# A routed feed-forward and attention kernel: scratch rows ordered by partition, gates of the last blocks worked out in block 6, block 1 turned inside block 0

## The chip, the cores and the metric

The kernel runs on one core of one Trainium2 chip. The metric is the device time of one launch in microseconds (us); each kernel was run several times and the median stands for it. The profile is one further execution.

Engines: TensorE (PE in the rows; PEld is its weight load), VectorE (DVE), ScalarE (ACT), GpSimd (POOL), SyncE (SP). SP and ACT issue plain DMA transfers; GpSimd issues indirect ones (gathers and scatters of rows by a list of indices).

## The reference

Three layers on x of 4 x 256 tokens with 256 features: half a mixture-of-experts feed-forward, attention, and the same feed-forward again.

```
x = x + 0.5 * ffn(layernorm(x))
x = x + attention(layernorm(x))       # 16 heads of 16, causal
x = x + 0.5 * ffn(layernorm(x))

ffn: logits = x @ router.T                     # 8 experts
     the best 2 experts of each token, gates = softmax of their 2 logits
     for each expert: a, b = split(x @ w_in.T) # 2 x 512
                      o = (silu(a) * b) @ w_out.T
                      sum += gate * o
     result = sum + bias
```

## The kernel before

Tokens lie in tiles of 128 on the partitions (8 tiles, in pairs); TensorE does all products in split precision (each operand as a high and a low part, three products). A feed-forward pass `ffn(f)`, f = 0 or 1, has these stages:

1. **Normalise and store.** The normalised rows `xn` (in the `arena` tile, or `xn_late`) are stored by ACT to `xn_scratch` in memory (L696, one transfer of 1 MB, semaphore `xn_stored`). In the first pass SP has by then issued the loads of weights (four of 1 MB for `w_raw`, 4 KB rows; two of 0.5 MB for `w_out`, 1 KB rows). In memory row `i * 128 + p` is token p of tile i.
2. **Route** (DVE L879 to L973, TensorE `route`). Each of the 2048 (token, expert) pairs gets a place in 23 blocks of 128 rows, each block of one expert. One-hot tiles (`row_hot`, `blk_hot`, `blk_pair`) are multiplied on TensorE (L1267) to give the pair's number at each place; from it come `gather_row` (which signals `plan_ready`) and `scatter_row`. `past` and `block_expert` give the expert of each block. Then the gates (L960 to L964) and, for the last two blocks, `live`, `slot_token` and `gate_row` (L966 to L973, signal `slots_ready`).
3. **Blocks.** GpSimd waits for `plan_ready` and `xn_stored`, gathers the rows of four blocks ahead (L509) and goes on by one for each block; a gather into a buffer waits until TensorE has turned the block that was in it. TensorE turns a block (`turn_block`), projects it in two halves (`project`, results a and b), turns the gated product (`turn_gated`) and multiplies by the second weights (`combine`), the three of them interleaved over neighbouring blocks. ACT copies the high parts out (`copy_xT`, `silu`, `copy_gT`, `split_out`, `copy_y`), DVE the low parts (`copy_xT_low`, `gated`, `split_out_low`, `copy_gT_low`, and in the first pass `split_low` of the expert weights). GpSimd scatters each block's result to `y_scratch` (L515). SP waits for the gathers of blocks 0 and 1 before it issues more weight loads. At block 6 GpSimd adds the bias to x (L503), at block 10 it gathers the gates of the last two blocks.
4. **Adding up.** The first 21 blocks go through `y_scratch`; when the last scatter has landed, SP loads them back to `y_in` (which lies in `w_out`) with eight transfers of 256 KB, one for each pair of tiles and each choice k, L436. DVE adds rows times gate to x (`add_rows`, L1021), ACT scales others (L627) that TensorE adds through an identity (`add_scaled`, L1351) on top of the last two blocks, which it spreads by one-hot tiles (`spread`, L1337). DVE adds TensorE's sum to x (`settle`, L1032); in the first pass the layer norm for attention follows, in the second SP stores the output.

`weigh_slots`, in the diff, is new; it is called in DVE's `body`.

## Time and profile before

| | |
|---|---|
| median of 3 runs | 437.04 us (435.76 to 438.95) |
| the profiled execution | 440.74 us, of which 438.6 us are its span |
| busy share of the span | PE 93%, PEld 76%, DVE 69%, ACT 59%, POOL 56% |
| DMA | 38.90 MB, 25738 packets; HBM read 29.37 MB, written 9.19 MB |
| the chain that ended last | PE 65%, DVE 12%, DMA 10%, issue 5%, ACT 3%, POOL 2% |

Times in the rows are microseconds from the start of the span. A timeline row has the start, the duration, engine, line of the kernel, operation, what it writes and reads, and in brackets how long the engine was idle before it and what ended that. SPq and ACTq are the instruction queues that issue transfers. The first pass runs from the start to about 159, attention to about 293, the second pass to the end. DMA queue q1 is SP's, q10 ACT's, q0 GpSimd's.

### The profile page before, as it was taken

What the parts mean: (1) busy time and instruction counts of PE and PEld (TensorE: products, weight loads), DVE (VectorE), ACT (ScalarE), POOL (GpSimd) and SP (SyncE); (2) the same over time, 40 slices, a digit from 0 to 9 for tenths busy, and PEclk for the clock granted to TensorE, in tenths of its full rate; (3) what the DMA queues carried; (4) which work ended last, traced back from release to release, by engine and by line L of the source; (5) the groups of instructions that cost most, each with busy time, mean ns of one, the idle gap of its engine ahead of it and who ended that gap; (6) DMA issues with size and microseconds to landing.
All of it is one profiled execution on the core that took longest, in us unless ns stands there. A gap on an engine that the chain in (4) does not pass through costs nothing.

```text
span 438.6 us, 10176 instructions
## 1 busy us (share of the span) xinstructions
PE 408.5 (93%) x2911; PEld 333.9 (76%) x2912; DVE 300.8 (69%) x613; ACT 257.1 (59%) x638; POOL 247.7 (56%) x307
## 2 busy tenths in 40 slices
PE   7768999999999889799999999888799999999996
PEld 4536888888888867588887888764488888888884
DVE  6767996865556697777677676966365575556566
ACT  2706885555655455788787787822155655655552
POOL 5136445866467349657777577210365586754850
PEclk9679999999999999989999999996999999999999
DMA  8929931111211630000000000007551212112136
GB/s 278 371 68 347 389 100 59 47 51 60 59 48 36 190 109 1 1 1 2 4 1 0 0 0 0 1 1 252 153 184 49 62 37 72 60 48 52 44 103 208
DMA packets 25738, 38.90 MB, mean 89 GB/s; under 512 B 3056, under 2 KB 20720, under 8 KB 25712
## 3 DMA queue, kind: packets, MB, share of 16 engines
q1 hardware_dynamic: 19088, 24.41, 16.3%
q0 software_dynamic: 4544, 12.07, 9.4%
q10 hardware_dynamic: 2080, 2.10, 1.4%
q8 instruction: 14, 0.23, 0.2%
q14 instruction: 12, 0.10, 0.1%
HBM read 29.37 MB, written 9.19 MB: 88 GB/s over the span
## 4 chain that ended last, share of the span: by engine, by line
PE 65%; DVE 12%; DMA 10%; issue 5%; ACT 3%; POOL 2%; SPq 1%; DVEq 0%; ACTq 0%; POOLq 0%
PE bank L1301 24%; PE bank L1323 12%; PE bank L1459 7%; PE bank L1470 4%; PE bank L1311 3%; DMA xn_scratch<-arena 3%; PE bank L1224 3%; DMA w_out<-y_scratch 3%; PE bank L1426 2%; PE bank L1277 2%; PE bank L1506 2%; DMA arena<-xn_scratch,gather_row 2%; DVE w_lo L876 1%; DMA y_scratch<-arena,scatter_row 1%; PE bank L1460 1%
## 5 line engine op out<-in xcount | busy, mean ns | idle before, releaser
L509 POOL DMA_INDIRECT arena<-xn_scratch,gather_row x46 | 50.8, 1105 | 72.7 <-PE bank L1277 42.1
L515 POOL DMA_INDIRECT y_scratch<-arena,scatter_row x42 | 60.2, 1434 | 34.3 <-ACT arena L681 31.2
L1301 PE MATMUL bank<-w_hi,xT_hi 128*128 x184 | 62.6, 421 | 1.2 <-ACT xT_hi L640 1.2
L990 DVE TENSOR_TENSOR wo_lo<-w_out,wo_hi 128x1024 fp32r<-128x1024 f32 x46 | 60.8, 1321 | 4.1 <-PE bank L1323 1.9
L995 DVE TENSOR_TENSOR gT_lo<-bank,gT_hi 128x512 fp32r<-128x512 f32 x46 | 31.7, 689 | 39.3 <-ACT gT_hi L655 39.2
L1301 PE MATMUL bank<-w_hi,xT_lo 128*128 x184 | 58.1, 397 | 0.0
L1301 PE MATMUL bank<-w_lo,xT_hi 128*128 x184 | 57.8, 395 | 0.0
L593 POOL TENSOR_TENSOR k_head<-k_hi,head_mask 128x256 fp32r<-128x256 f32 x64 | 38.7, 625 | 29.1 <-PE bank L1460 22.2
L648 ACT ACTIVATE arena<-bank 128x512 f32<-128x512 f32 x46 | 27.5, 598 | 45.7 <-PE bank L1301 45.7
L670 ACT ACTIVATE wo_hi<-w_out 128x1024 fp32r x46 | 48.8, 1060 | 6.0 <-issue 4.1
L979 DVE TENSOR_TENSOR xT_lo<-bank,xT_hi 128x256 fp32r<-128x256 f32 x46 | 19.5, 424 | 39.0 <-ACT xT_hi L640 38.9
L1459 PE MATMUL bank<-k_head,xT_hi 128*128 128x256 f32 (+1 forms) x128 | 40.4, 397 | 1.9 <-ACT probs L778 1.2
L1301 PEld LDWEIGHTS bank<-w_hi,xT_lo 128*128 128x128 f32 x184 | 35.1, 191 | 8.0
L1301 PEld LDWEIGHTS bank<-w_lo,xT_hi 128*128 128x128 f32 x184 | 34.9, 190 | 8.2
L593 POOL TENSOR_TENSOR k_head<-k_lo,head_mask 128x256 fp32r<-128x256 f32 x64 | 38.3, 618 | 0.6 <-DVE k_lo L1105 0.6
L681 ACT ACTIVATE arena<-bank 128x256 f32<-128x256 f32 x42 | 16.2, 385 | 37.0 <-PE bank L1323 37.0
L770 ACT ACTIVATE probs<-bank,neg_max 128x256 f32<-128x256 f32 x64 | 29.9, 478 | 8.6 <-DVE neg_max L1118 8.6
L788 ACT ACTIVATE pT_hi<-bank 128x384 f16<-128x384 f32 x64 | 28.1, 487 | 11.3 <-PE bank L1470 10.5
L1323 PE MATMUL bank<-wo_hi,gT_hi 128*128 128x256 f32 x184 | 33.0, 302 | 1.4 <-ACT gT_hi L655 1.4
L1224 PE MATMUL bank<-ones 128*128 128x512 f16 x95 | 31.1, 479 | 3.3 <-POOL ident L462 1.8
L1131 DVE SCALAR_TENSOR_TENSOR pT_lo<-bank,pT_hi 128x384 f16<-128x384 f32 x64 | 32.4, 548 | 0.6
L1004 DVE TENSOR_TENSOR arena<-arena,bank 128x512 f32<-128x512 f32 x46 | 31.2, 678 | 1.0 <-issue 0.9
(180 smaller groups left out, 968.8 us busy)
## 6 DMA issues: line engine op xcount, KB each, us to landing
w_raw<-in_win_t SPq DMA_DIRECT2D x8, 1024.0 KB, 9.7
w_out<-in_wout_t SPq DMA_DIRECT2D x16, 512.0 KB, 8.0
w_out<-y_scratch SPq DMA_DIRECT2D x16, 256.0 KB, 4.9
xn_scratch<-arena ACTq DMA_DIRECT2D x2, 1024.0 KB, 8.7
x<-in_x SPq DMA_DIRECT2D x4, 256.0 KB, 3.6
out<-x SPq DMA_DIRECT2D x4, 256.0 KB, 2.1
arena<-xn_scratch,gather_row POOLq DMA_INDIRECT x46, 3.5
y_scratch<-arena,scatter_row POOLq DMA_INDIRECT x46, 3.0
```

Of the source, the lines that this page charges most:

```text
L509: pool.indirect_dma_start(out=xb[j % 2][:, :], out_offset=None, in_=xn_dram, in_offset=bass.IndirectOffsetOnAxis(ap=gather_row[:, j:j + 1] ...
L515: pool.indirect_dma_start(out=y_dram, in_=y[j % 2][:, :], in_offset=None, out_offset=bass.IndirectOffsetOnAxis(ap=scatter_row[:, j:j + 1], ...
L593: ins = pool.tensor_tensor(k_head[s % KSLOTS][:, part, hh, :], k[:, c, :].bitcast(F32), head_mask[:, h % HPC:h % HPC + 1].to_broadcast([P, ...
L670: act.activation(wo_hi[u][:, :, :], w_out[:, bass.ds(e, 1), :, :].rearrange("p o c d -> p (o c) d"), ACT.Copy)\
L990: dve.tensor_tensor(wo_lo[:, :, :], w_out[:, bass.ds(e, 1), :, :].rearrange("p o c d -> p (o c) d"), wo_hi[u][:, :, :].bitcast(F32), ALU.s ...
L995: dve.tensor_tensor(gT_lo[:, :, :], bank[4][:, :].rearrange("p (c t) -> p c t", c=HK), gT_hi[:, :, :].bitcast(F32), ALU.subtract).then_inc ...
L1004: dve.tensor_tensor(g[:, :], sa[:, :], bank[2 + u][:, :], ALU.mult).then_inc(g_done, 1)
L1131: dve.scalar_tensor_tensor(pT_lo[u][:, :, :], bank[3 + hh][:, 0:3 * P].rearrange("p (k t) -> p k t", k=3), P_SCALE, pT_hi[u][:, :, :], ALU ...
L1224: pe.matmul(bank[into][:, :], ones[:, :], bc(ones[:, :], 1, [P, 512 // P, P]), start=True, stop=True)
L1301: last = pe.matmul(bank[2 * half + u][:, :], tok[u][:, k, :], wts[:, bass.ds(e, 1), k, half * H:(half + 1) * H], start=(part == 0 and k == ...
L1323: last = pe.matmul(bank[y_bank(j)][:, 0:D], tok[:, c, :], wts[:, c, :], start=(part == 0 and c == 0), stop=(part == 2 and c == HK - 1))
L1459: pe.matmul(to, q[:, 1 if tail else 0, :], keys[:, part, :, 0:width], start=(n == 0), stop=False)
```

## The change

In words:

- Rows in `xn_scratch` and `y_scratch` are numbered by partition first (`p * 8 + i` instead of `i * 128 + p`), so a partition's 8 tiles are one run of 8 KB in memory. The store of `xn` writes such runs. `pair_id` and `tile_edge` are made to fit; `tile_edge` costs one more small operation on GpSimd among the constants.
- `y_in` is laid out by choice, then tile. A pair of tiles is loaded by one transfer of 512 KB for both choices, in runs of 2 KB; four transfers instead of eight.
- The gates, `live` and `slot_token` move out of `route` to `weigh_slots`, which DVE runs at the end of block 6. The gates in memory are ordered like the pairs, so `gate_p`, `gate_q` and `gate_row` go, and the gather of gates takes `pair_i` itself.
- In `route`, `past` comes after `blk_pair`.
- On TensorE block 1 is turned between the two halves of block 0's projection, not after them.

```diff
--- before.py
+++ after.py
...
@@ -177,7 +177,7 @@
 
         y_experts = TOPK * TILES // HK
         assert LAST + y_experts <= SCATTERED - FULL + 1 and LAST * TILES * P <= (SCATTERED - LAST * 2 - FULL + 1) * HK * D
-        y_in = view(w_out_words, LAST * HK * D, [TILES, TOPK, D])[0]
+        y_in = view(w_out_words, LAST * HK * D, [TOPK, TILES, D])[0]
 
         wr = sb("wr", [P, DK, E])
         bias_half = sb("bias_half", [P, D])
...
@@ -372,9 +369,9 @@
 
         x_rows = x_in.rearrange("b (j p) d -> p (b j) d", p=P)
         out_rows = out.rearrange("b (j p) d -> p (b j) d", p=P)
-        xn_rows = xn_dram.rearrange("(i p) d -> p i d", p=P)
-        gate_rows = gate_dram.rearrange("(p q) o -> p (q o)", p=P)
-        y_rows = y_dram[0:TOPK * T, :].rearrange("(k i p) d -> p k i d", p=P, k=TOPK)
+        xn_rows = xn_dram.rearrange("(p i) d -> p i d", p=P)
+        gate_rows = gate_dram.rearrange("(k p i) o -> p k (i o)", p=P, k=TOPK)
+        y_rows = y_dram[0:TOPK * T, :].rearrange("(k p i) d -> p k i d", p=P, k=TOPK)
 
 
         @block.sync
@@ -426,15 +423,14 @@
                     pass_on_w_out()
 
                 sp.wait_ge(slots_ready, f + 1)
-                sp.dma_start(gate_rows, gate[:, :, :].rearrange("p k i -> p (k i)")).then_inc(gates_stored, 16)
+                sp.dma_start(gate_rows, gate[:, :, :]).then_inc(gates_stored, 16)
 
                 sp.wait_ge(rows_zeroed, 16 * LAST * (f + 1))
                 sp.wait_ge(scattered[0], 16 * S_EVEN * (f + 1))
                 sp.wait_ge(scattered[1], 16 * S_ODD * (f + 1))
                 for i in range(TPAIRS):
-                    for k in range(TOPK):
-                        sp.dma_start(y_in[:, 2 * i:2 * i + 2, k, :], y_rows[:, k, 2 * i:2 * i + 2, :])\
-                            .then_inc(y_loaded[i], 16)
+                    two = slice(2 * i, 2 * i + 2)
+                    sp.dma_start(y_in[:, :, two, :], y_rows[:, :, two, :]).then_inc(y_loaded[i], 16)
                 if f == 0:
 
                     sp.wait_ge(wo_lo_ready, BLOCKS)
@@ -484,9 +480,10 @@
             inverse_root(0, 1)
             iota(col[:, :], [[1, P]], 0, 0)
             inverse_root(0, 2)
-            iota(tile_edge[:, :], [[P, TILES]], 0, 0)
+            iota(tile_edge[:, :], [[1, TILES]], 0, 0)
+            then(pool.tensor_scalar(tile_edge[:, :], tile_edge[:, :], 1.0 / TILES, None, ALU.mult))
             inverse_root(0, 3)
-            iota(pair_id[:, :].rearrange("p (k i) -> p k i", k=TOPK), [[T, TOPK], [P, TILES]], 1, 1)
+            iota(pair_id[:, :].rearrange("p (k i) -> p k i", k=TOPK), [[T, TOPK], [1, TILES]], 1, TILES)
             iota(trash_id[:, :], [[P, BLOCKS]], TOPK * T + 1, 1)
             then(pool.memset(neg_mask[:, :], 0.0))
             select(neg_mask[:, :], [[-1, P]], 0, 1, ALU.is_ge, NEG)
@@ -531,7 +528,7 @@
                 pool.wait_ge(gates_stored, 16 * (f + 1))
                 for k in range(LAST):
                     pool.indirect_dma_start(out=slot_gate[:, k:k + 1], out_offset=None, in_=gate_dram,
-                                            in_offset=bass.IndirectOffsetOnAxis(ap=gate_row[:, k:k + 1], axis=0))\
+                                            in_offset=bass.IndirectOffsetOnAxis(ap=pair_i[:, SCATTERED + k:SCATTERED + k + 1], axis=0))\
                         .then_inc(gates_gathered, 16)
 
             def mark_tokens(f, k, half):
...
@@ -937,15 +934,15 @@
                 one_hot_rows(slice(PAIRS // 2, PAIRS))
                 dve.wait_ge(route_step, block_at)
                 block_at = mark(dve.tensor_tensor(block_of[:, :], block_of[:, :], blk_i[:, :], ALU.add))
-                dve.wait_ge(route_step, end_at)
-                past_at = mark(dve.tensor_tensor(past[:, :, :], bc(end_block[:, :], 1, [P, BLOCKS, E]),
-                                                 bc(block_no[:, :], 2, [P, BLOCKS, E]), ALU.is_le))
                 dve.wait_ge(route_step, block_at)
                 then(dve.tensor_tensor(blk_hot[:, :, :], bc(block_of[:, :], 2, [P, PAIRS, BLOCKS]),
                                        bc(block_no[:, :], 1, [P, PAIRS, BLOCKS]), ALU.is_equal))
                 dve.tensor_tensor(blk_pair[:, :, :], blk_hot[:, :, :], bc(pair_id[:, :], 2, [P, PAIRS, BLOCKS]), ALU.mult)\
                     .then_inc(hot_ready, 1)
 
+                dve.wait_ge(route_step, end_at)
+                past_at = mark(dve.tensor_tensor(past[:, :, :], bc(end_block[:, :], 1, [P, BLOCKS, E]),
+                                                 bc(block_no[:, :], 2, [P, BLOCKS, E]), ALU.is_le))
                 dve.wait_ge(route_step, past_at)
                 then(dve.tensor_reduce(block_expert_f[:, :], past[:, :, :], AX_X, ALU.add))
                 dve.tensor_scalar(block_expert[:, :], block_expert_f[:, :], float(E - 1), None, ALU.min)
@@ -957,20 +954,19 @@
                 then(dve.scalar_tensor_tensor(empty[:, :], pair_of, 0.0, trash_id[:, :], ALU.is_equal, ALU.mult))
                 dve.scalar_tensor_tensor(scatter_row[:, :], pair_of, 1.0, empty[:, :], ALU.subtract, ALU.add)\
                     .then_inc(scatter_ready, 1)
+
+            def weigh_slots(f):
+
                 dve.wait_ge(e1_ready, f + 1)
                 then(dve.tensor_scalar(den[:, :], e1[:, :], 1.0, None, ALU.add))
                 then(dve.reciprocal(den[:, :], den[:, :]))
                 then(dve.tensor_scalar(gate[:, 0, :], den[:, :], 0.5, None, ALU.mult))
                 then(dve.tensor_tensor(gate[:, 1, :], gate[:, 0, :], e1[:, :], ALU.mult))
 
-                dve.tensor_scalar(live[:, :], pair_of[:, SCATTERED:BLOCKS], 0.0, None, ALU.is_gt)
-                dve.tensor_scalar(gate_p[:, :], pair_i[:, SCATTERED:BLOCKS], P - 1, PAIRS.bit_length() - 1, ALU.bitwise_and,
-                                  ALU.logical_shift_left)
-                dve.tensor_scalar(gate_q[:, :], pair_i[:, SCATTERED:BLOCKS], P.bit_length() - 1, None, ALU.logical_shift_right)
+                dve.tensor_scalar(live[:, :], bank[7][:, SCATTERED:BLOCKS], 0.0, None, ALU.is_gt)
                 each = [P, LAST, TILES]
-                then(dve.tensor_tensor(slot_token[:, :, :], bc(gather_row[:, SCATTERED:BLOCKS], 2, each),
-                                       bc(tile_edge[:, :], 1, each), ALU.subtract))
-                dve.tensor_tensor(gate_row[:, :], gate_p[:, :], gate_q[:, :], ALU.bitwise_or).then_inc(slots_ready, 1)
+                dve.scalar_tensor_tensor(slot_token[:, :, :], bc(gather_row[:, SCATTERED:BLOCKS], 2, each), 1.0 / TILES,
+                                         bc(tile_edge[:, :], 1, each), ALU.mult, ALU.subtract).then_inc(slots_ready, 1)
 
             def copy_xT_low(f, j, u):
                 dve.wait_ge(xT_hi_ready, f * BLOCKS + j + 1)
...
@@ -1079,6 +1075,8 @@
                         split_out_low(f, j + 1, 1 - u, e)
                     if f == 0 and isinstance(j, int) and j + EARLY < E:
                         split_low(j + EARLY)
+                    if isinstance(j, int) and j == PEELED - 1:
+                        weigh_slots(f)
 
                 for j in range(PEELED):
                     body(j, j % 2)
...
@@ -1374,9 +1372,9 @@
                 warm(WARM_TURNED[f], 4)
                 first = expert(0)
                 project(f, 0, 0, 0, first)
+                turn_block(f, 1, 1, base[1] + 1)
                 project(f, 0, 0, 1, first)
                 second = expert(1)
-                turn_block(f, 1, 1, base[1] + 1)
                 project(f, 1, 1, 0, second)
                 turn_gated(f, 0, 0)
                 project(f, 1, 1, 1, second)
```

Left out: the count of constants (21 to 22), the declarations of `gate_p`, `gate_q` and `gate_row`, and the index order `y_in[:, k, t, :]` and the count of 16 instead of 32 a transfer pair at the uses of `y_in`.

## Rows read from the trace of the kernel before

**Rows 1.** The chain that ended last, whole run: start us, us, what.

```profile
11.24 12.97 DMA xn_scratch<-arena
24.28 0.83 issue
...
147.04 5.47 DMA w_out<-y_scratch
...
309.20 2.92 DMA arena<-xn_scratch,gather_row
...
426.79 6.32 DMA w_out<-y_scratch
```

**Rows 2.** The DMA view, windows 15:16, 20:21 (packets, MB, share), then 296:297 us.

```profile
q10 hardware_dynamic: 48, 0.05, 13.8%
...
q1 hardware_dynamic: 90, 0.29, 72.5%
q10 hardware_dynamic: 96, 0.10, 27.4%
...
xn_scratch<-arena ACTq DMA_DIRECT2D x1, 1024.0 KB, 4.5
```

**Rows 3.** Stretches: us, busy time by engine, PEclk, DMA share, GB/s.

```profile
10.00:11.00 1.00, 1.00 (x11) 0.97 (x10) 0.74 (x3) 0.15 (x1) 0.86 (x4) 1.00 1.03 418
...
297.00:298.00 1.00, 1.00 (x6) 0.81 (x5) 0.69 (x7) 0.00 (x0) 0.00 (x0) 0.50 1.00 346
303.00:305.00 2.00, 2.00 (x7) 0.68 (x5) 2.00 (x10) 0.58 (x2) 0.00 (x0) 0.55 1.07 360
...
427.00:428.00 1.00, 1.00 (x11) 1.00 (x10) 0.62 (x2) 0.46 (x1) 0.00 (x0) 1.00 0.89 232
```

**Rows 4.** Timeline of DVE, 20 to 25 us: start, us, instruction.

```profile
20.78 0.34 DVE L941 TENSOR_TENSOR past<-end_block,block_no 128x184 f32<-128x184 f32 x1
21.04 0.53 DVE L944 TENSOR_TENSOR arena<-block_of,block_no 128x368 f32<-128x368 f32 x1
...
23.03 0.18 DVE L956 TENSOR_SCALAR gather_row<-pair_i 128x23 int32<-128x23 int32 x1
...
23.42 0.16 DVE L961 TENSOR_SCALAR den<-e 128x8 f32<-128x8 f32 x1
...
24.67 0.16 DVE L973 TENSOR_TENSOR gate_row<-gate_p,gate_q 128x2 int32<-128x2 int32 x1
```

**Rows 5.** Timeline, blocks 0 and 1 of the first pass, 34 to 42 us.

```profile
35.42 0.72 PE L1301 MATMUL bank<-w_hi,xT_hi 128*128 x2 [0.66 <-ACT xT_hi L640]
...
36.21 0.69 DVE L1004 TENSOR_TENSOR arena<-arena,bank 128x512 f32<-128x512 f32 x1 [0.57 <-issue]
...
41.04 0.74 PE L1323 MATMUL bank<-wo_hi,gT_lo 128*128 128x256 f32 x4 [0.87 <-DVE gT_lo L995]
```

**Rows 6.** The same stage of the second pass, 316 to 318 us: block 1's first matmuls.

```profile
316.99 0.72 PE L1301 MATMUL bank<-w_hi,xT_hi 128*128 x2 [0.56 <-ACT xT_hi L640]
```

**Rows 7.** Timeline of DVE, block 7 of the first pass, 75 us.

```profile
75.50 0.69 DVE L995 TENSOR_TENSOR gT_lo<-bank,gT_hi 128x512 fp32r<-128x512 f32 x1 [1.20 <-ACT gT_hi L655]
```

**Rows 8.** Timeline, end of the first pass, 151 to 160 us.

```profile
152.54 0.88 DVE L1021 SCALAR_TENSOR_TENSOR x<-w_out,gate,x 128x256 f32<-128x256 f32 x2 [1.42 <-DMA w_out<-y_scratch]
...
156.41 2.00 PE L1351 MATMUL bank<-w_out,ident 128*128 128x256 f32 x8 [0.35 <-ACT w_out L627]
...
159.21 0.67 DVE L1032 TENSOR_TENSOR x<-x,bank 128x512 f32<-128x512 f32 x1
```

**Rows 9.** Timeline, end of the second pass, 423 to 437 us.

```profile
423.31 3.95 SPq L436 DMA_DIRECT2D w_out<-y_scratch  x8
...
428.80 2.15 PE L1337 MATMUL bank<-gated_last,slot_hot 128*128 128x256 f32 x16
...
433.13 0.91 ACT L627 ACTIVATE w_out<-w_out,gate 128x256 f32<-128x256 f32 x2 [0.44 <-DMA w_out<-y_scratch]
...
435.36 0.69 DVE L1032 TENSOR_TENSOR x<-x,bank 128x512 f32<-128x512 f32 x1 [0.66 <-PE bank L1351]
```

More of the change, by code:

```diff
@@ L53 @@
 EARLY = 3
-CONSTS = 21
+CONSTS = 22
 IDENT_CONSTS = 3
@@ L216, in build @@
         live = sb("live", [P, LAST])
-        gate_p = sb("gate_p", [P, LAST], I32)
-        gate_q = sb("gate_q", [P, LAST], I32)
-        gate_row = sb("gate_row", [P, LAST], I32)
         slot_gate = sb("slot_gate", [P, LAST])
@@ L550, in ffn @@
                     for i in range(TPAIRS):
-                        pool.wait_ge(y_loaded[i], 16 * TOPK)
+                        pool.wait_ge(y_loaded[i], 16)
                 for j in range(AHEAD):
@@ L624, in scale_rows @@
                 for i, k in PE_ROWS[f]:
-                    act.wait_ge(y_loaded[i], 16 * TOPK * (f + 1))
+                    act.wait_ge(y_loaded[i], 16 * (f + 1))
                     for t in (2 * i, 2 * i + 1):
-                        ins = act.activation(y_in[:, t, k, :], y_in[:, t, k, :], ACT.Copy, scale=gate[:, k, t:t + 1])
+                        ins = act.activation(y_in[:, k, t, :], y_in[:, k, t, :], ACT.Copy, scale=gate[:, k, t:t + 1])
                     ins.then_inc(y_scaled, 1)
@@ L1013, in add_rows @@
             def add_rows(f, i, k):
-                dve.wait_ge(y_loaded[i], 16 * TOPK * (f + 1))
+                dve.wait_ge(y_loaded[i], 16 * (f + 1))
                 n = DVE_ROWS[f].index((i, k))
@@ L1020, in add_rows @@
                 for t in (2 * i, 2 * i + 1):
-                    ins = dve.scalar_tensor_tensor(x[:, t, :], y_in[:, t, k, :], gate[:, k, t:t + 1], x[:, t, :],
+                    ins = dve.scalar_tensor_tensor(x[:, t, :], y_in[:, k, t, :], gate[:, k, t:t + 1], x[:, t, :],
                                                    ALU.mult, ALU.add)
@@ L1350, in add_scaled @@
                     for t in (2 * i, 2 * i + 1):
-                        last = pe.matmul(acc(t), ident[:, :], y_in[:, t, k, :], start=False, stop=(last_of and t % 2 == 1),
+                        last = pe.matmul(acc(t), ident[:, :], y_in[:, k, t, :], start=False, stop=(last_of and t % 2 == 1),
                                          skip_group_check=True)
```

## The prediction

> **What bounds the kernel now.** I read the chain of waits first, to see which transfers stand on it. The pass blocks are TensorE work back to back (blocks repeat every 4.9 us and TensorE does not wait inside them), so no transfer inside them is worth anything. Three transfers of the scratch tensors are on the chain by name [rows 1]: the store of xn in the first pass, 12.97 us from its issue at 11.24, and the two loads of y at the passes' ends, 5.47 and 6.32 us. The second pass's gather starts at 309.20 with no store ahead of it: there the plan, not the store, comes last. So the change can win at four kinds of place: the store of the first pass, the plan, the opening of blocks 0 and 1 (both passes), and the two ends.
>
> Then the DMA view by window and the stretches. A queue's packet here is one contiguous run: the store's are 96 for 0.10 MB, 1 KB each [rows 2]. While the store competes with the weight loads, the two queues move nearly one packet for one: 90 against 96 in the same microsecond, although the loads' packets are up to 4 KB and the store's 1 KB [rows 2]. Alone, the second store needs 4.5 us [rows 2]. In the stretches, 1 KB packets alone run at 346 and 360 GB/s, 4 KB packets at 418, all with the DMA engines full; the y load has a stretch at 232 GB/s for a reason that the profile does not show [rows 3]. Last the timelines of the places that the change touches [rows 4 to 9].
>
> **The change, part by part.**
>
> *Store in 8 KB runs, first pass.* If the queues go on trading packet for packet [rows 2], a store of 8 KB packets gets most of the bandwidth instead of a fifth to a half of it. The store's first 48 packets moved only in the microsecond from 15 on, 4 us after its issue [rows 2]. From 16 on 1.05 MB at 346 to 418 GB/s, with an eighth to a half as much of the loads between, is 3 to 5 us: landed by 21, before the plan (gather_row written at 23.03 + 0.18 = 23.2 [rows 4]). GpSimd now comes free at 24.28 and spends 0.83 more before it issues [rows 1]; I keep those 0.83. The gather then starts at about 23.25 + 0.83 instead of 25.11: **0.95 us**. The low end is 0, if the store still lands with the backlog; the high end 1.8, if the 0.83 goes too. The loads behind it move the same bytes and are needed over 5 us later than they land. The second store is hidden by the plan (296.0 + 4.5 = 300.5, the gather at 309.20 [rows 1, 2]): 0.
>
> The Trainium skill (DMA: Bandwidth & Descriptors, "Queues, rings and completion order") says that an engine round-robins between the queues it has work for, a packet at a time; the one-for-one count above agrees.
>
> *Order of `past`.* L941 stands ahead of the one-hot of the blocks and costs 0.26 us, start to start [rows 4], of which the wait for `block_of` would take 0.12 anyway. But it and its reduction now lie between the one-hot and `pair_i`, and on my count of the issue order DVE comes to `pair_i` when TensorE's 16 matmuls are done, 0.05 earlier than now. Ends 0 and 0.14; I take **0.05 in each pass**.
>
> *Gates in block 6.* DVE leaves nine small operations between 23.42 and 24.83 [rows 4]; nothing on the chain waits for them there (the gather does not need them). Now seven of them, about 1.1 us, come behind block 6's `wo_lo`, where DVE idles 1.20 us before block 7's L995 [rows 7]. So they fit, with 0.1 to spare; if L995 were late by 0.3 for register loads, TensorE wants its result only as the last third of the combine. **0**, at worst 0.2 each pass. What moves along: the store of the gates waits on SP, with nothing behind it but the y load, 60 us later, and its 32-byte runs are 256 packets; the gates' gather on GpSimd stands at block 10.
>
> *Block 1 turned between block 0's halves.* Second pass: TensorE waits 0.56 us before block 1's first matmul, for ACT's copy of the turned block [rows 6]. Turned 1.4 us earlier, ACT copies it right behind block 0's silu, under the second half. The two transposes cost the same, wherever they stand. **0.55** (ends 0.3 and 0.6; block 1's gather has landed long before). First pass: the same wait is 0.66, but the bound behind it is DVE: its L1004 of block 0 starts at 36.21 after the split of block 1, then come `wo_lo` and a weight split, and TensorE waits for `gT_lo` until 41.04 [rows 5]. With block 1 copied about 1.4 earlier, L1004 is limited by block 0's second half (later by the 0.4 of the moved transposes) and starts near 34.9. The DVE chain comes 1.2 to 1.3 earlier, ACT's about 0.6 with slack. I take **1.1** (ends 0.55 and 1.3).
>
> *The y load: 4 transfers in 2 KB runs.* Price of a packet from two rows: 1024 B at 360 GB/s over 16 engines is 45.5 ns, 4096 B at 418 is 157 ns [rows 3], so 8 ns fixed and 37 ns per KB; 2 KB is then 83 ns, or 397 GB/s. The fixed part of a transfer comes from the lone store: 4.5 - 1.05 MB / 346 = 1.5 us [rows 2, 3]. The load of 2.10 MB in the second pass is then 1.5 + 5.3 = 6.8 us from its issue at 423.31, landing at 430.1; before, 1.5 + 5.8 would have done, and it took until 433.11 [rows 1, 9], so 2.5 us went into the slow stretches. If these stay, the new load lands at 432.6. Between the two I expect about 431.3. What is late next: TensorE. Its spread ends at 428.80 + 2.15 = 430.95 and the twelve matmuls of the rows to add take 0.25 each (2.00 for 8), so it is done at 433.95 if ACT's 0.91 for the last pair begins by 432.0. Now it is done just before 435.36, when DVE adds the last pair [rows 8, 9]. So the cap is 1.3, reached if the last pair lands by 432.0; floor 0. I take **1.1**. In the first pass DVE waits 1.42 for the second pair at 152.54 and is then busy to 159.21 with hardly a gap [rows 8]; the second pair at 397 GB/s lands before 151.1. Cap 1.4, floor 0; I take **1.15**.
>
> The Trainium skill (DMA: Bandwidth & Descriptors, "Why small descriptors are slow (HBM only)") puts the overhead at about 3 cycles a packet beside one cycle per 32 bytes. That is 35 against 67 cycles for 1 and 2 KB, a gain of 4% or, as an estimate, 0.25 us a load. It speaks against most of this term; the rows give 9%, since 418 against 360 is more than that rule allows.
>
> *Sum.* 0.95 + 2 x 0.05 + (1.1 + 0.55) + (1.15 + 1.1) = **4.95 us**. The profiled execution took 440.74 us (span 438.6), so 435.8; the median of the runs is 3.7 lower, and the sum taken from it gives 437.04 - 4.95 = **432.1 us**.
>
> **The rivals.**
>
> 1. *The y load stays slow.* The slow stretch (232 GB/s with the engines 0.89 busy [rows 3]) is then of the memory, not of the packets. For it: packets there take up to 1.5 times as long as the same ones elsewhere, with no other queue active. Against it: issue of eight transfers takes 3.95 us [rows 9], now four. The last pair lands at 432.6 and both ends give 0.6: 4.95 - 2.25 + 1.2 = 3.9, 433.1 us. With the small overhead alone, 0.25 an end, it is 3.2: 433.8 us. The page on descriptors says the latter; the row at 418 speaks against it.
> 2. *The store lands with the backlog all the same*, because its descriptors are cut small again, or served behind the loads. For it: it began to move 4 us late. Against: 90 against 96. Only 0.95 goes: 433.1 us.
> 3. *Other side: strided runs are slow.* The old layout reads the rows of a tile in a row; the new one takes 2 KB pieces 8 KB apart, and gathers and scatters hit rows 8 KB apart. If these collide in memory, the load runs slower throughout. At 232 GB/s, the slowest stretch of now, it takes 1.5 + 9.0 us, 0.7 more than the 9.8 of now; the ends lose 0.7 each instead of giving 2.25, and the sum is 2.7 - 1.4: still 1.3 faster, 435.7. To be no faster, each end must lose 1.35, or 11.15 us a load: 217 GB/s. To be slower by 1% each must lose 3.55, a rate of 177 GB/s. Gathers are no danger in the blocks: each has a wait of over 4 us to spare. Against it: no row shows a cost of distance, and packets elsewhere go at full speed in 4 KB pitches.
> 4. *The gates are in the way.* L995 of block 7 late beyond the third of the combine, 0.2 to 0.5 in each pass: 432.5 to 433.1 us.
>
> **How the numbers follow.** Forecast 0.52 (own range 431.0 to 433.0); rival 1 0.22 (432.8 to 434.3); rival 2 0.09 and rival 4 0.05 (432.5 to 433.5); more than the sum, if the 0.83 goes or the ends overlap better, 0.05 (430 to 431); rival 3 0.07, mostly 434.5 to 438, beyond its point in 0.02. The rounds of the kernel before themselves spread over 3 us, which widens both ends. The range is 430.2 to 435.5. About 1%, 4.4 us, is what a measurement of this kernel can tell from no change: faster is below 432.7. That holds four fifths of the forecast, a tenth of rival 1 and all of the "more" case: 0.50; slower 0.03; the rest 0.47.
>
> **What would show it.** Right: no wait of GpSimd for the store in the first pass, the gather at about 24.1; block 1's first matmul with no idle time before it in both passes; the y load landed 8.0 us or less after its first issue, and DVE's last add of a pass held by TensorE alone. Wrong: a store that lands at 24; L995 of block 7 with TensorE waiting behind it; a stretch under 260 GB/s in the y load, above all at 2 KB packets; gathers with more than 4 us to landing in the middle of a pass. The whole falls if a transfer that I call hidden (attention weights behind the y load, expert weights behind the store) shows up as a releaser.

## The result and the profile after

| kernel | median of its runs, us | ratio to before [95% interval] |
|---|---|---|
| before, beside it | 438.0 (4 runs) | |
| changed | 444.11 (443.28 to 447.75) | 1.0149 [1.0101, 1.0197] |

The change makes the kernel slower by 1.5%, 6 us, where the prediction had 432.1 us and 430.2 to 435.5. The profiled execution took 444.56 us with a span of 442.8; TensorE is busy for 409.8 us of it (93%), as long a share as before. Ratios here and below leave out executions over 1.5% longer than the fastest of the same kernel; the medians beside them are of all executions.

The chain of waits of the changed kernel, its transfers only (start us, us, what):

```profile
24.07 3.60 DMA arena<-xn_scratch,gather_row
139.09 3.02 DMA y_scratch<-arena,scatter_row
142.16 4.09 DMA w_out<-y_scratch
305.24 3.55 DMA arena<-xn_scratch,gather_row
425.25 3.01 DMA y_scratch<-arena,scatter_row
429.76 7.56 DMA w_out<-y_scratch
```

The store of xn is gone from it [rows 1]. The second pass's gather starts 3.96 us earlier than before (305.24 against 309.20 [rows 1]), so the kernel has won what it should up to there: the forecast is 3.3 us, and some 1.2 of the 3.96 come from a higher clock at the first block (see under "The turn"). The second pass then loses: its last scatter, at 420.24 before, starts at 425.25. I took the start of `gT_lo` (L995 before, L991 after) as a mark in each block. In us:

| stretch | before | after | difference |
|---|---|---|---|
| start to first gather | 25.11 | 24.07 | -1.04 |
| to `gT_lo` of block 0 | 15.20 | 12.35 | -2.85 |
| to `gT_lo` of block 22 | 107.44 | 107.88 | +0.44 |
| to the last `settle` of the pass | 11.46 | 10.90 | -0.56 |
| attention and plan, to the second gather | 149.99 | 150.04 | +0.05 |
| to `gT_lo` of block 0 | 10.60 | 12.06 | +1.46 |
| to `gT_lo` of block 22 | 105.67 | 113.18 | **+7.51** |
| to the last `settle`, and the end | 13.13 | 12.32 | -0.81 |

Blocks 0 to 5 and 10 to 22 of the second pass take what they took before. 7.44 of the 7.51 lie between `gT_lo` of block 6 and of block 9: 22.11 us instead of 14.67. The timeline of the changed kernel there, 348 to 361 us:

```profile
349.59 1.59 POOL L512 DMA_INDIRECT y_scratch<-arena,scatter_row  x1 [0.87 <-ACT arena L678]
...
350.25 0.17 DVE L961 TENSOR_SCALAR den<-e 128x8 f32<-128x8 f32 x1
...
350.45 0.20 DVE L962 RECIPROCAL den<-den 128x8 f32<-128x8 f32 x1
...
350.69 5.11 DVE L963 TENSOR_SCALAR gate<-den 128x8 f32<-128x8 f32 x1
...
351.20 4.56 POOL L500 TENSOR_TENSOR x<-x,bias_half 128x2048 f32<-128x2048 f32 x1
...
356.97 0.69 DVE L991 TENSOR_TENSOR gT_lo<-bank,gT_hi 128x512 fp32r<-128x512 f32 x1 [0.70 <-issue]
...
357.71 1.22 PE L1321 MATMUL bank<-wo_hi,gT_lo 128*128 128x256 f32 x4 [4.45 <-DVE gT_lo L991]
...
358.74 1.05 PE L1299 MATMUL bank<-w_hi,xT_hi 128*128 x2
```

An operation on 8 numbers a partition takes 5.11 us. It starts beside GpSimd's scatter, the scatter ends at 351.18, the bias addition starts at 351.20 and ends at 355.76, and VectorE's operation ends at 355.80. `gT_lo` of block 7 stands behind it (after three more small operations and 0.70 us of issue), and TensorE waits 4.45 us for that. The stretches behind it (columns as in [rows 3]):

```profile
355.00:358.00 3.00, 0.28 (x1) 0.29 (x2) 2.23 (x7) 0.00 (x0) 1.75 (x2) 0.81 0.14 27
358.00:361.00 3.00, 3.00 (x10) 2.52 (x11) 1.81 (x2) 0.38 (x1) 1.28 (x1) 0.50 0.07 25
361.00:364.00 3.00, 3.00 (x11) 2.45 (x10) 0.69 (x1) 1.96 (x3) 0.24 (x1) 0.55 0.13 44
364.00:367.00 3.00, 3.00 (x21) 2.71 (x20) 1.74 (x3) 1.06 (x3) 1.14 (x2) 1.00 0.11 37
```

After the idle time the granted clock is 0.50 and 0.55 (1.2 GHz) for some 6 us: two matmuls of a projection take 1.05 us instead of 0.62. 4.45 us of waiting and some 3.0 us lost at half clock make the 7.44.

The first pass has the same order of work on VectorE and loses only 0.44 us over its blocks. Its rows in the changed kernel:

```profile
69.69 1.59 POOL L512 DMA_INDIRECT y_scratch<-arena,scatter_row  x1 [0.86 <-ACT arena L678]
71.32 0.89 POOL L560 TENSOR_SCALAR bias_half<-bias_half 128x256 f32<-128x256 f32 x1
72.72 4.61 POOL L500 TENSOR_TENSOR x<-x,bias_half 128x2048 f32<-128x2048 f32 x1 [0.51 <-issue]
```

```profile
70.79 0.47 DVE L963 TENSOR_SCALAR gate<-den 128x8 f32<-128x8 f32 x1
...
71.57 0.21 DVE L968 SCALAR_TENSOR_TENSOR slot_token<-gather_row,tile_edge 128x16 f32<-128x16 int32 x1
...
74.28 4.14 DVE L986 TENSOR_TENSOR wo_lo<-w_out,wo_hi 128x1024 fp32r<-128x1024 f32 x1
```

Here GpSimd halves the bias first (L560), and the addition starts only at 72.72, when the gates are done. What it holds instead is `wo_lo`, as in the kernel before. That was there to be read before the prediction; two places of the timeline of the kernel before:

```profile
76.23 4.63 POOL L503 TENSOR_TENSOR x<-x,bias_half 128x2048 f32<-128x2048 f32 x1
...
77.95 3.99 DVE L990 TENSOR_TENSOR wo_lo<-w_out,wo_hi 128x1024 fp32r<-128x1024 f32 x1
...
82.00 0.74 PE L1323 MATMUL bank<-wo_lo,gT_hi 128*128 128x256 f32 x4 [0.36 <-DVE wo_lo L990]
...
353.62 4.65 POOL L503 TENSOR_TENSOR x<-x,bias_half 128x2048 f32<-128x2048 f32 x1
...
356.43 2.94 DVE L990 TENSOR_TENSOR wo_lo<-w_out,wo_hi 128x1024 fp32r<-128x1024 f32 x1
```

`wo_lo` takes 1.23 us in every other block. Beside the addition it ends at 81.94 and 359.37, some 1.1 us after the addition, as if it had stood still until then. "TensorE does not wait inside them", as the prediction says of the blocks, passed over what this costs: TensorE waits 0.36 us for it in the first pass, and blocks 6 to 9 take 15.43 us there against 14.67 in the second pass. The Trainium skill (SBUF — State Buffer, "SBUF: two separate sides") says that VectorE and GpSimd share a pair of ports under an exclusive lock and that the loser blocks for the whole instruction. These rows agree, and VectorE's operations that read PSUM (`gT_lo`, `xT_lo`) ran beside the same addition at their usual 0.69 and 0.42 us.

### The profile page after: what moved, and what is told of

It is laid out like the page before. It is cut to its first block, busy times and chain, and to the rows that moved or that the text cites. A ratio compares the mean times of both kernels' runs of the same rounds, so it can differ in the third digit from the quotient of the medians.

```text
span 442.8 us, 10163 instructions
## 1 busy us (share of the span) xinstructions
PE 409.8 (93%) x2911; PEld 334.1 (75%) x2912; DVE 304.0 (69%) x607; ACT 257.2 (58%) x638; POOL 249.0 (56%) x308
## 4 chain that ended last, share of the span: by engine, by line
PE 61%; DVE 20%; DMA 6%; issue 5%; ACT 3%; POOL 2%; DVEq 1%; ACTq 0%; SPq 0%; POOLq 0%
PE bank L1299 22%; PE bank L1321 11%; PE bank L1457 6%; PE bank L1468 4%; PE bank L1309 3%; DMA w_out<-y_scratch 3%; PE bank L1424 2%; DVE w_lo L873 2%; PE bank L1222 2%; PE bank L1275 2%; DVE wo_lo L986 2%; PE bank L1504 2%; DMA arena<-xn_scratch,gather_row 2%; DMA y_scratch<-arena,scatter_row 1%; PE bank L1458 1%
## 5 line engine op out<-in xcount | busy, mean ns | idle before, releaser
L506 POOL DMA_INDIRECT arena<-xn_scratch,gather_row x46 | 49.5, 1076 | 74.0 <-PE bank L1275 45.7
L512 POOL DMA_INDIRECT y_scratch<-arena,scatter_row x42 | 62.5, 1487 | 37.1 <-ACT arena L678 34.3
L1299 PE MATMUL bank<-w_hi,xT_hi 128*128 x184 | 63.5, 427 | 0.0
L986 DVE TENSOR_TENSOR wo_lo<-w_out,wo_hi 128x1024 fp32r<-128x1024 f32 x46 | 59.2, 1287 | 4.4 <-PE bank L1321 2.6
L991 DVE TENSOR_TENSOR gT_lo<-bank,gT_hi 128x512 fp32r<-128x512 f32 x46 | 31.7, 690 | 41.7 <-ACT gT_hi L652 40.2
L1321 PE MATMUL bank<-wo_hi,gT_lo 128*128 128x256 f32 x184 | 31.0, 291 | 5.7 <-DVE gT_lo L991 5.6
L1222 PE MATMUL bank<-ones 128*128 128x512 f16 x95 | 32.3, 494 | 3.0 <-POOL ident L458 1.8
```

The source lines that it names most:

```text
L506: pool.indirect_dma_start(out=xb[j % 2][:, :], out_offset=None, in_=xn_dram, in_offset=bass.IndirectOffsetOnAxis(ap=gather_row[:, j:j + 1] ...
L512: pool.indirect_dma_start(out=y_dram, in_=y[j % 2][:, :], in_offset=None, out_offset=bass.IndirectOffsetOnAxis(ap=scatter_row[:, j:j + 1], ...
L986: dve.tensor_tensor(wo_lo[:, :, :], w_out[:, bass.ds(e, 1), :, :].rearrange("p o c d -> p (o c) d"), wo_hi[u][:, :, :].bitcast(F32), ALU.s ...
L991: dve.tensor_tensor(gT_lo[:, :, :], bank[4][:, :].rearrange("p (c t) -> p c t", c=HK), gT_hi[:, :, :].bitcast(F32), ALU.subtract).then_inc ...
L1222: pe.matmul(bank[into][:, :], ones[:, :], bc(ones[:, :], 1, [P, 512 // P, P]), start=True, stop=True)
L1299: last = pe.matmul(bank[2 * half + u][:, :], tok[u][:, k, :], wts[:, bass.ds(e, 1), k, half * H:(half + 1) * H], start=(part == 0 and k == ...
```

## The experiments

The theory: the whole loss is that the gates now stand just ahead of and beside GpSimd's bias addition of block 6. The rival: the new row order costs something (gathers, scatters, loads), and the gates cost little. Twelve kernels in three groups; the kernels of a group ran on one chip beside the kernel before (medians 438.74, 439.49 and 438.98 us there).

**Gates out of block 6.** The gates back in the plan, all else new:

```diff
             def ffn(f):
                 route(f)
+                weigh_slots(f)
...
-                    if isinstance(j, int) and j == PEELED - 1:
-                        weigh_slots(f)
```

> The changed kernel with the gates worked out at the end of the routing again, as in the kernel before; everything else of the change stays. Theory 1 (the gates in block 6 are the whole loss: a small DVE operation waits behind GpSimd's bias addition in the second pass): the 4.45 us stall of TensorE, the slow clock behind it and the 0.4 us of the first pass go, about 7.9 us, so 436 us against 438 before. Theory 2 (the new row order is slow, the stall only hides it): not below the kernel before, 439 us or more.

Measured: 434.88 us (10 runs), ratio 0.9921 [0.9881, 0.9961].

**Only the gates moved**, on the kernel before (they become a `weigh_slots`, with their old operations, called in block 6):

```diff
+                    if isinstance(j, int) and j == PEELED - 1:
+                        weigh_slots(f)
```

> The kernel before with only the gates moved to the end of block 6. Theory 1: it is the change that loses; if both passes meet GpSimd's bias addition 438 + 7.5 + up to 4, if one of them does 445, and if neither does 438.5 to 439, since whether DVE gets in between two GpSimd instructions is a matter of some 0.05 us. Theory 2 (row order): 438.5 whatever happens, as the order of rows is the old one.

Measured: 445.21 us (4 runs), ratio 1.0125 [1.0084, 1.0166]. Its timeline, 350 to 358 us:

```profile
352.71 5.11 DVE L967 TENSOR_SCALAR gate<-den 128x8 f32<-128x8 f32 x1
...
353.23 4.55 POOL L503 TENSOR_TENSOR x<-x,bias_half 128x2048 f32<-128x2048 f32 x1
```

With the old row order and the old transfers the same operation takes the same 5.11 us, and blocks 6 to 9 of the second pass lose 6.68 us. The move alone makes a loss, and undoing it alone takes the loss away. The sizes agree only roughly: by the ratios the move costs 5.5 us on the kernel before, and undoing it in the changed kernel gives 10.0. The hold explains 7.4 of that, and the changed kernel's profiled execution has another 2 us at the opening of its second pass, of which more below; the rest is within the intervals, each some 2 us to either side.

**The gates one block earlier, or the addition two blocks later.** `j == PEELED - 2` for the gates; for the addition:

```diff
-                    if j == 6:
+                    if j == 8:
```

> The changed kernel with the gates at the end of block 5 instead of block 6; GpSimd then issues only a scatter beside them. Theory 1: no operation of DVE waits for the bias addition in this place, 436 us as in the kernel with the gates in the routing, within 0.7 us of it. Rival (any small DVE work between the blocks costs, by the 0.7 to 0.8 us before the next high-minus-low step): 1 to 1.5 us more than with the gates in the routing, 437.5 us.

Measured: 434.92 us (4 runs), ratio 0.9914 [0.9890, 0.9938]; L963 takes 0.17 us.

> The changed kernel with the gates still in block 6, but GpSimd's bias addition moved from block 6 to block 8. Theory 1: the gates wait at most 0.5 us for the scatter's issue, no 5 us operation; 436 to 437 us. Rival (the gates wait for the scatters, not for the addition; or the addition costs as much wherever it stands): 440 us or more.

Measured: 434.72 us (4 runs), ratio 0.9906 [0.9888, 0.9925]; L963 takes 0.17 us, with the gates still in block 6. Its second pass:

```profile
347.06 1.59 POOL L512 DMA_INDIRECT y_scratch<-arena,scatter_row  x1 [0.87 <-ACT arena L678]
...
348.16 0.17 DVE L963 TENSOR_SCALAR gate<-den 128x8 f32<-128x8 f32 x1
```

L963 starts 0.49 us before the scatter ends, exactly as in the changed kernel (350.69 and 351.18), and is not held. So the scatter alone does not hold it: the addition behind the scatter does, although its row begins only 0.51 us after L963 does. Neither the gates' work nor their place costs anything by itself, only gates and addition side by side.

**Half the addition in block 6**, the other half in block 8:

```diff
+                    if j == 8:
+                        add_bias(2 * f, bias_half, 2, 2)
                     if j == 6:
...
-                        add_bias(2 * f, bias_half)
+                        add_bias(2 * f, bias_half, 0, 2)
```

> The new kernel with one half of the bias addition (two of four pairs of tiles, about 2.4 us on GpSimd) left in block 6 and the other half in block 8. If VectorE is held by whatever runs on GpSimd, from the scatter to the end of what follows without a gap, the third small operation of the gates takes 2.8 us in the second pass instead of 5.11, and the loss shrinks from 7.4 to about 3 us or less: 436 to 439. If any addition behind the scatter costs the whole stall, it stays at 444.

Measured: 437.66 us (10 runs), ratio 0.9978 [0.9935, 1.0021]. Its second pass:

```profile
347.89 2.95 DVE L965 TENSOR_SCALAR gate<-den 128x8 f32<-128x8 f32 x1
...
348.41 2.39 POOL L500 TENSOR_TENSOR x<-x,bias_half 128x1024 f32<-128x1024 f32 x1
...
352.76 0.75 PE L1323 MATMUL bank<-wo_hi,gT_lo 128*128 128x256 f32 x4 [2.30 <-DVE gT_lo L993]
...
353.35 0.63 PE L1301 MATMUL bank<-w_hi,xT_hi 128*128 x2
```

The held time goes down with the addition (2.95 against 5.11), again to 0.04 us after its end. The loss goes down further, from 7.44 to 2.55 us: after an idle time of 2.30 us the matmuls go on at full clock (0.63), after 4.45 they did not. That separates the two parts of the loss. The kernel as a whole can't be told from the kernel before: the rest of the change gives 3.5 to 4.1 us, and 2.55 of it are lost again.

**The addition in four instructions** of a quarter each, one behind the other in block 6:

```diff
-                        add_bias(2 * f, bias_half)
+                        for i in range(TPAIRS):
+                            add_bias(2 * f, bias_half, i, 1)
```

> The new kernel with GpSimd's addition of the bias cut into four instructions of a quarter the size, gates still in block 6. If VectorE is held only for one instruction of GpSimd, the first small operation of the gates takes at most 1.3 us instead of 5.11, later ones may be held once more, and the kernel takes 435 to 437 us. If the whole addition has to end first, it stays at 444.

Measured: 442.12 us (10 runs, 438.99 to 443.79), ratio 1.0040 [1.0005, 1.0076].

```profile
348.88 1.59 POOL L512 DMA_INDIRECT y_scratch<-arena,scatter_row  x1 [0.86 <-ACT arena L679]
350.50 4.95 POOL L500 TENSOR_TENSOR x<-x,bias_half 128x512 f32<-128x512 f32 x4
...
349.98 5.51 DVE L964 TENSOR_SCALAR gate<-den 128x8 f32<-128x8 f32 x1
```

My expectation was wrong. VectorE is held through all four, 5.51 us, not for one of them, and TensorE waits 4.83 us; the second pass loses 7.57 us in these blocks. The first pass gains 0.9 against the changed kernel: there `wo_lo` began between two of the quarters and took 1.64 us. The timed runs are 2 us better than the changed kernel's by the medians and 4.8 by the ratios, and of that only the 0.9 is explained. The profiled execution (443.79 us) is the longest of the ten; whether others escape the hold is open.

**The gates ahead of `wo_lo`**, still in block 6:

```diff
                         gated(f, j + 1, 1 - u)
+                        if isinstance(j, int) and j == PEELED - 1:
+                            weigh_slots(f)
                         split_out_low(f, j + 1, 1 - u, e)
...
-                    if isinstance(j, int) and j == PEELED - 1:
-                        weigh_slots(f)
```

> The new kernel with the gates still in block 6, but ahead of wo_lo instead of behind it, so that VectorE has done them before the scatter of GpSimd begins. The small operations then take 0.2 us each and wo_lo (two operands in SBUF) falls beside the scatter and the bias addition: it takes 5 to 6 us in the second pass. TensorE wants wo_lo in the second third of the combine, so some of the stall stays: 437 to 444. If the gates themselves were the cost, nothing changes from 444.

Measured: 441.19 us (10 runs), ratio 1.0046 [1.0006, 1.0086].

```profile
348.35 0.17 DVE L963 TENSOR_SCALAR gate<-den 128x8 f32<-128x8 f32 x1
...
348.85 5.30 DVE L968 SCALAR_TENSOR_TENSOR slot_token<-gather_row,tile_edge 128x16 f32<-128x16 int32 x1
...
354.07 1.21 DVE L986 TENSOR_TENSOR wo_lo<-w_out,wo_hi 128x1024 fp32r<-128x1024 f32 x1
```

The time is as expected, the place is not: the last of the small operations is the one that is held, and `wo_lo` comes behind it. TensorE waits 3.60 us for `wo_lo` and blocks 6 to 9 lose 5.13 us. Which of these instructions of VectorE is caught makes no difference, only what stands behind it.

**The addition in quarters, spread** over blocks 8, 11, 13 and 14 (the halving of the bias at block 7):

```diff
-                    if j == 6:
...
+                    if j in (8, 11, 13, 14):
+                        add_bias(2 * f, bias_half, (8, 11, 13, 14).index(j), 1)
```

> The new kernel with the bias addition in four quarters of 1.2 us behind the scatters of blocks 8, 11, 13 and 14. No operation of VectorE is held for over 2.5 us in either pass, and the 0.8 us that the held wo_lo costs in the first pass and 0.2 in the second are gone: 434.7 - 0.9 = 433.8 us. If the holding costs TensorE nothing, 434.7.

Measured: 433.14 us (4 runs, 430.87 to 437.56), ratio 0.9845 [0.9756, 0.9933]. No operation of VectorE takes over 2.5 us. Blocks 0 to 22 of the first pass take 106.70 us, 0.70 less than with the undivided addition in block 8 (107.40); in the second pass they take 105.86 against 105.67. This has the lowest ratio of all, 1.6% below the kernel before, on three executions; that it beats the 0.9906 of the undivided addition is not settled by the intervals. Nor do the profiled executions settle it: of their difference of 1.9 us, 1.5 lie in attention and the plan behind it, where the two kernels are the same (147.55 us against 149.07). That stretch takes between 147.55 and 150.09 us in the fourteen profiles, and no edit goes with it.

**Only the turn**, on the kernel before (the diff of the section on the change):

> The kernel before with one edit: block 1 turned between the halves of block 0's projection. By the parts of the new kernel's traces (block 0's low half of the gated product 1.65 earlier after its gather in the first pass, 0.65 in the second) this alone gives 2.3 us. By the prediction it gives 1.1 + 0.55 = 1.65 us. If the gain needs the earlier store, under 1 us.

Measured: 436.15 us (10 runs), ratio 0.9933 [0.9896, 0.9970], 2.9 us by the ratio. From the first gather to `gT_lo` of block 0 the first pass takes 13.10 us, the second 9.69.

**Only the row order, the store and the loads:** turn, `past` and gates as before.

> The new row order with its 8 KB store, the y load in four transfers and the simpler gather of gates, but the turn, the place of past and the gates in the plan as before. Store 1.0 us, y load 0.5 in the first pass and 0.5 to 0.8 in the second: 2.0 to 2.3 us faster than before. By the prediction's terms it would be 0.95 + 1.15 + 1.1 = 3.2 us. If the new row order costs anything in the blocks, less than 1.5 us.

Measured: 437.12 us (10 runs), ratio 0.9946 [0.9917, 0.9975], 2.4 us by the ratio. Blocks 0 to 22 of the second pass take 105.67 us, the same as before to a hundredth: the order of the rows costs the gathers and scatters nothing there. In the first pass they take 107.89, 0.44 more than before, as in the changed kernel. 0.33 of that lie between blocks 6 and 9 and belong to the bias addition: in the kernels with the new order and the undivided addition in block 6 it starts after 0.5 us of issue behind L560, and `wo_lo` beside it takes 4.36 us instead of 3.99. With the addition in block 8 the difference is gone (107.40). Where the 0.5 us of issue come from is open.

**More warming ahead of the first gather** (nine instead of six matmuls, addition in block 8):

```diff
-WARM_START, WARM_RANKS, WARM_PLAN, WARM_TURNED = 12, (11, 18), (6, 6), (4, 4)
+WARM_START, WARM_RANKS, WARM_PLAN, WARM_TURNED = 12, (11, 18), (9, 6), (4, 4)
```

> The new kernel with the bias addition moved from block 6 to block 8, and nine instead of six warming matmuls ahead of the plan's one in the first pass. With the addition in block 8 alone it took 434.7 us. If the warming holds TensorE at full clock when the first gather lands, block 0's opening gives up to 1.1 us more, 433.6; if not, the same 434.7 within 0.5.

Measured: 437.40 us (10 runs, 433.91 to 439.88), ratio 0.9972 [0.9931, 1.0013]. The clock did not hold: at 28.64 us the first matmuls take 1.34 and 1.05 us, as with six (1.27 and 1.06). The kernel is not faster but slower than with six, in the profiled execution mostly through a wait at block 12 of the first pass that no edit explains (7.24 us instead of 4.79 from `gT_lo` to `gT_lo`).

**Eight loads of y in 2 KB runs** (addition in block 8):

```diff
-                    sp.dma_start(y_in[:, :, two, :], y_rows[:, :, two, :]).then_inc(y_loaded[i], 16)
+                    for k in range(TOPK):
+                        sp.dma_start(y_in[:, k, two, :], y_rows[:, k, two, :]).then_inc(y_loaded[i], 16)
```

> The new kernel with the bias addition in block 8, and each pair of tiles of y loaded in two transfers, one a choice, in the same 2 KB runs: eight issues (3.95 us) instead of four (1.90). If the first pair lands late because one transfer of 512 KB ramps up slower than two of 256 KB, the first rows come 0.5 us earlier after the issue (3.6 instead of 4.2 us) and the kernel takes 434.2; if the number of issues costs, the last pair lands 0.3 to 0.6 later and it takes 435.1.

Measured: 439.19 us (10 runs), ratio 1.0001 [0.9968, 1.0035]. The end of the second pass, first of the changed kernel, then of this one:

```profile
428.33 1.90 SPq L433 DMA_DIRECT2D w_out<-y_scratch  x4
...
432.54 0.88 DVE L1017 SCALAR_TENSOR_TENSOR x<-w_out,gate,x 128x256 f32<-128x256 f32 x2 [0.99 <-DMA w_out<-y_scratch]
433.74 1.85 DVE L1017 SCALAR_TENSOR_TENSOR x<-w_out,gate,x 128x256 f32<-128x256 f32 x4
```

```profile
421.11 3.66 SPq L434 DMA_DIRECT2D w_out<-y_scratch  x8
...
429.68 0.88 DVE L1018 SCALAR_TENSOR_TENSOR x<-w_out,gate,x 128x256 f32<-128x256 f32 x2 [0.87 <-DMA w_out<-y_scratch]
...
433.23 0.69 DVE L1029 TENSOR_TENSOR x<-x,bank 128x512 f32<-128x512 f32 x1 [0.63 <-PE bank L1350]
```

From the start of the last scatter to the end of the last `settle` the second pass takes 15.89 us here. The old eight loads with 1 KB runs took 14.99, 15.24 and 15.81; of the ten kernels with four loads of 2 KB runs nine took 14.53 to 15.01, and the tenth (the gates ahead of `wo_lo`) 15.94. So longer runs alone, with eight loads, show no gain in this execution, but one execution of the four loads was as slow: whether the number of transfers or the length of the runs gives the gain is not settled. Of the kernel's 4 us against the same with four loads, 1.3 are this end. Most of the rest lies in waits at block 12 of the first pass and block 13 of the second (7.37 and 6.51 us from `gT_lo` to `gT_lo`, elsewhere 4.8 and 4.9), the first of which the kernel with more warming has too. ScalarE and VectorE stop together there, for 4.1 and 3.1 us; what they wait for the records don't show, and it stays open.

## Why the prediction was wrong

**The gates (forecast 0, at worst 0.2 each pass; measured 7.4 us in the second pass).** This is the step that failed. "So they fit" rested on the durations that the operations had in the plan, where GpSimd is idle. The prediction counted what else is due on VectorE in that slot, and not what runs on GpSimd in it, though "each queue that it is moved past" was the right question. Had it been asked, the rows of `wo_lo` at 3.99 and 2.94 us beside the addition gave the price: the gates come behind `wo_lo` of block 6, the scatter starts 0.5 us into that and the addition follows it with no gap in the second pass, so up to 4.65 us, with `gT_lo` behind. Against 1.2 us of room that is over 3 us of waiting on TensorE. (Six operations moved, not seven; they take the 1.1 us that was forecast, in the kernel with the addition in block 8.) Rival 4 named the place and gave it 0.05 at 0.2 to 0.5 us a pass; its mechanism, register loads, was not what costs: the 0.70 us before L991 are covered where nothing is held (TensorE goes on without a gap in the kernel with the addition in block 8), and are part of the 4.45 here only because the hold ends so late.

**The store (forecast 0.95).** Right in mechanism. The changed kernel at 16 to 17 us:

```profile
q10 hardware_dynamic: 46, 0.38, 88.8%
q1 hardware_dynamic: 68, 0.07, 18.6%
```

46 packets for 0.38 MB are 8 KB each, against 68 of the loads. The store lands 9.2 us after its issue at 11.35, at 20.6, where 21 was forecast (before: 24.21), and at 19.2 to 21.3 in the other kernels with the new order. GpSimd's first gather starts at 24.07 and waits for `gather_row`, no more for the store. The 0.83 us of issue stayed. The gather starts at 23.97 to 24.07 in all ten kernels with the new order and `past` moved, and at 25.11, 25.07 and 24.53 in the three with the old store: 0.87 on the mean, `past` included. (The prediction's own numbers, 25.11 less 23.25 and 0.83, give 1.03 and not 0.95.) `past` itself can be read from the plan: from the start of the addition into `block_of` to that of `gather_row` it is 2.33 to 2.35 us in the four kernels with `past` in its old place and 2.29 in the ten with the new one, in both passes. That is 0.04, forecast 0.05. Now that the store is early, the plan sets the gather: the kernel with only the row order gathers at 24.43, its plan having come to `block_of` 0.3 us later than in the others.

**The turn (forecast 1.1 + 0.55).** From gather to `gT_lo` of block 0 the three kernels without it take 15.20, 15.01 and 14.63 us in the first pass and 10.58 to 10.62 in the second; with it and with TensorE at the same clock 13.10 to 13.85 and 9.69 to 9.97. That is 1.4 and 0.8: a little more than forecast on the mean, though the first pass's 1.4 is 1.9 to 2.1 with the old store and 0.8 to 1.2 with the new one. The changed kernel's own profile hides the second (12.06) and flatters the first (12.35; 12.28 in the kernel with eight loads), both by the clock: in the first pass its projection ran at full clock from 28.82 (0.73 us a pair, before 1.06), in the second at half. The second pass's opening, changed kernel, then the one with the addition in block 8:

```profile
308.83 0.49 PE L1275 MATMUL bank<-ident,arena 128*128 128x128 f32 x2 [2.36 <-DMA arena<-xn_scratch,gather_row]
309.12 1.91 PE L1222 MATMUL bank<-ones 128*128 128x512 f16 x4
```

```profile
308.00 0.44 PE L1275 MATMUL bank<-ident,arena 128*128 128x128 f32 x2 [1.89 <-DMA arena<-xn_scratch,gather_row]
308.28 1.03 PE L1222 MATMUL bank<-ones 128*128 128x512 f16 x4
```

The gather landed 0.5 us later in the first, TensorE idled 2.36 us and the same four matmuls took 1.91 instead of 1.03. The kernel with the addition in four shows it again (2.39, 1.91), the other kernels, idle for 1.65 to 1.91 us there, do not. It is worth 2 us and stands in two of the fourteen profiles, ahead of the place where these two kernels differ from the others, so I take it for chance between executions. How many of the timed executions have it is not known.

**The loads of y (forecast 1.15 + 1.1).** A third of that: from the last scatter to the last `settle` 16.1 us instead of 16.3 in the first pass, and in the second, to its end, 14.8 instead of 15.35 (means of ten kernels with four loads and of three with the old ones), so 0.2 and 0.55. The mis-sized term of the second pass is the landing, "about 431.3", 8.0 us after the first issue: ACT takes up the last pair 8.5 to 9.0 us after it in nine of the ten, before 9.0 to 9.8. The slow stretch stayed (252 GB/s at 433 to 434 us of the changed kernel with the engines 0.88 busy), which was rival 1. And the first rows come later with four loads, 4.0 to 4.3 us after the first issue against 3.5 to 4.1; from the second addition on VectorE then works nearly without a gap to the end (1.85 us for the four additions at 433.74). The cap of 1.3 counted TensorE alone. In the first pass the wait of 1.42 us for the second pair did go, as forecast, but 0.98 us of waiting for the first pair took its place (0.23 before).

**The sum.** Without the hold the terms come to 0.87 + 1.4 + 0.8 + 0.2 + 0.55 = 3.8 us, less up to 0.4 for the later bias addition of the first pass, and the three kernels that remove it are faster by 3.5 to 4.1 us by their ratios. The forecast was 4.95; without the hold it would have been 1 us too good, with the right sign. Two experiments alone give 2.9 + 2.4 = 5.3, the same within their intervals. Rival 3, strided runs, does not show: the blocks of the second pass take the same as before to a hundredth, and nine of the ten ends with four loads are no slower than the old ones. So the prediction failed by one term put at nothing; the terms that it had came out right in sign, the loads at a third of their size.

## What to carry to other kernels

Before moving small operations of VectorE into a "free" slot, list what GpSimd runs in that slot, its scatters and gathers too, and look in the trace for a VectorE operation with SBUF operands that takes longer than its twins there: that surplus is the price, whatever the size of what is moved. What decides is the operation queued behind the held one: `wo_lo` had some 2 us of room (1.7 us more cost nothing, 2.8 us more cost 0.8), `gT_lo` of the next block had one. Large additions on GpSimd belong in pieces, apart from each other, where a held operation has room behind it.

## What the hardware showed that I had not expected

- The hold does not depend on the size of what is held: 128x8 (5.11 us), 128x16 (5.30) and 128x1024 (3.99) all ended 0.04 us, or their own working time, after GpSimd's addition.
- It begins before the addition's own row and does not end with one instruction of GpSimd. L963 starts 0.51 us before the addition, beside a scatter that by itself does not hold it (0.17 us with the addition in block 8), and stands to the addition's end (5.11 us). Behind a scatter and four additions with no gap between them it stood for all four (5.51 us). Behind a scatter with L560 next it took 0.47 us, to the scatter's end, in the first pass, and the small operations after it ran beside L560 at 0.17 to 0.21. So it depends on what GpSimd has next, and not only on what its row shows as running; how, the rows don't show. The Trainium skill (same page and section as above) has the winner hold for its instruction; these two points are in these rows only.
- The length of an idle time alone does not tell whether TensorE's clock falls. In the blocks it was at half (1.2 GHz) after 4.84, 4.83, 4.45 and 3.60 us without a matmul, and at full after 2.30. At the openings it fell to half after 2.36 and 2.39 us (second pass) and after 2.21 (first pass, more warming). Where it fell, the wait cost more than itself: 7.44 us for 4.45, 6.68 for 4.84 and 5.13 for 3.60, against 2.55 for 2.30 where it held.
